# First chunk of a fused recommender kernel: tiles selected by 0/1 matmuls, dummy matmuls, loads issued two parts at a time

## The reference, cut to what matters

```python
e = stack([tbl_f[ids[:, f]] for f in range(39)], axis=1)     # (512, 39, 16)
x0 = xk = e
for idx, (W, b) in enumerate(((w0, b0), (w1, b1), (w2, b2))):
    z = relu(einsum('bhd,bkd,hks->bsd', x0, xk, W) + b[None, :, None])
    if idx != 2:
        xk = z[:, :64, :];  direct.append(z[:, 64:, :])
    else:
        direct.append(z)
z = sum(concatenate(direct, axis=1), axis=-1)
h = relu(concatenate([z, dense_ctx], axis=1) @ W_top1 + b_top1)
y = relu(h @ W_top2 + b_top2) @ W_top3
```

## Time and profile before

| | us |
|---|---|
| median of 3 runs (641.41 to 642.8) | 641.43 |
| profiled execution, device time | 643.21 |
| its span, first to last instruction | 641.4 |
| PE busy | 601.1 (94%) |
| DVE busy | 550.5 (86%) |
| POOL busy | 462.4 (72%) |
| ACT busy | 302.9 (47%) |
| mean granted TensorE clock | 0.987 |

### The profile page before, as it was taken

The page is one execution under the profiler, slowest core; times in us unless marked ns, Lnnn a source line. Parts: engine busy times, 40 slices in busy tenths (PEclk is TensorE's granted clock), DMA queues, the critical chain, the costliest instruction groups (busy, mean ns, idle before and its releaser), DMA issues.

```text
span 641.4 us, 7217 instructions
## 1 busy us (share of the span) xinstructions
PE 601.1 (94%) x1916; PEld 362.1 (56%) x1916; DVE 550.5 (86%) x509; ACT 302.9 (47%) x374; POOL 462.4 (72%) x293
## 2 busy tenths in 40 slices
PE   0258999999999999999999999999999999999998
PEld 0024565666666665656666665656566666656463
DVE  1456999999999999999999999999999999999540
ACT  2023555546454646445364546454454545455313
POOL 6807787878878787878878787878788787647230
PEclk9978999999999999999999999999999999999998
DMA  6798788796959494968769494959787693922000
GB/s 231 170 209 192 160 186 178 167 196 150 210 126 218 95 220 102 219 129 187 162 151 210 109 217 100 219 107 201 143 191 169 138 221 90 219 56 70 2 0 0
DMA packets 28431, 98.13 MB, mean 153 GB/s; under 512 B 8033, under 2 KB 16993, under 8 KB 20354
## 3 DMA queue, kind: packets, MB, share of 16 engines
q1 hardware_dynamic: 21297, 93.44, 66.0%
q0 software_dynamic: 5120, 1.32, 1.9%
q10 hardware_dynamic: 2001, 3.24, 1.5%
HBM read 94.14 MB, written 3.84 MB: 153 GB/s over the span
## 4 chain that ended last, share of the span: by engine, by line
PE 92%; DMA 2%; POOL 2%; DVE 2%; ACT 1%; issue 1%; SPq 1%; DVEq 0%; ACTq 0%
PE z L585 42%; PE z L591 13%; PE z L596 13%; PE z L593 13%; PE z L575 4%; PE z L579 2%; PE z L578 2%; PE d_products L649 1%; POOL gathered L397 1%; DMA x_rep<-x_rows 1%; DVE products L451 1%; PE z L624 1%; POOL low L342 0%; SPq L304 0%; DMA gathered<-in_tables,rows_sb 0%
## 5 line engine op out<-in xcount | busy, mean ns | idle before, releaser
L342 POOL TENSOR_TENSOR low<-products,high 128x1024 fp32r<-128x1024 f32 x128 | 303.9, 2391 | 112.8 <-ACT high L689 101.8
L451 DVE TENSOR_TENSOR products<-x_rep,xk 128x1024 f32<-128x1024 f32 (+1 forms) x258 | 333.0, 1337 | 25.8 <-ACT xk L673 17.9
L585 PE MATMUL z<-products,w_whole 128*128 128x512 f32 x640 | 301.6, 602 | 30.5 <-DVE products L451 30.5
L585 PEld LDWEIGHTS z<-products,w_whole 128*128 128x128 f32 x640 | 122.8, 192 | 136.3 <-issue 121.7
L689 ACT ACTIVATE high<-products 128x1024 fp32r<-128x1024 f32 x128 | 134.8, 1055 | 134.3 <-DVE products L451 121.8
L397 POOL DMA_INDIRECT gathered<-in_tables,rows_sb x160 | 157.8, 986 | 44.4 <-issue 41.3
L591 PE MATMUL z<-high,w_high 128*128 128x512 f32 x352 | 184.4, 524 | 2.6 <-ACT high L689 2.6
L593 PE MATMUL z<-high,w_low 128*128 128x512 f32 x352 | 138.9, 395 | 0.0
L596 PE MATMUL z<-low,w_high 128*128 128x512 f32 x352 | 110.1, 394 | 1.4 <-POOL low L342 1.3
L591 PEld LDWEIGHTS z<-high,w_high 128*128 128x128 f32 x352 | 66.7, 189 | 40.9 <-issue 24.8
L593 PEld LDWEIGHTS z<-high,w_low 128*128 128x128 f32 x352 | 66.7, 190 | 37.5 <-issue 26.8
(11 more groups left out here) (41 smaller groups left out, 156.2 us busy)
## 6 DMA issues: line engine op xcount, KB each, us to landing
x_rep<-x_rows SPq DMA_DIRECT2D x60, 768.0 KB, 14.9
x_rep<-x_rows SPq DMA_DIRECT2D x62, 512.0 KB, 6.4
x_rows<-gathered SPq DMA_DIRECT2D x15, 225.0 KB
x_rep<-x_rows SPq DMA_DIRECT2D x8, 384.0 KB, 8.3
x_rep<-in_w ACTq DMA_DIRECT2D x2, 1280.0 KB, 9.6
gathered<-in_tables,rows_sb POOLq DMA_INDIRECT x160
x_same<-x_rows SPq DMA_DIRECT2D x15, 78.0 KB
x_same<-x_rows SPq DMA_DIRECT2D x16, 64.0 KB
```

The lines of the kernel that those rows point to most:

```text
L342: ops.tensor_tensor(low[0:p, slot, 0:n, :], product(index, p, n), high[0:p, slot, 0:n, :].bitcast(fp32), ALU.subtract).then_inc(low_by[kin ...
L451: nc.vector.tensor_tensor(slots, rep, row.unsqueeze(1).broadcast_to([p, n, N]), ALU.mult).then_inc(made, 1 + pair)
L585: mm = nc.tensor.matmul(out, w_whole[0:p, at, i, :], product(index, p, n)[:, i, :], start=(first and i == 0), stop=(last and i == n - 1))
```

## The change

FIRST_PARTS becomes six parts, of which tiles 4 and 5 come first. The other tiles of layer 0 (SELECTED: 0, 1, 6, 2, 3) are, for the first chunk only, no longer read from `x0_rep`: PE multiplies `x0_same` by a 128 x 128 matrix of zeros and ones for each, so that the row wanted on each partition appears in a PSUM bank (`select`), and DVE multiplies that bank by `x0_same` (`multiply_selected`), one tile at a time. The five matrices are a new input `sel`, loaded by ACT's queue behind w1 and w2 into ring slot 0 of `products`. PE gets three dummy matmuls ahead of the selections, started when the gathers of chunk 0 are done, and three behind layer 0 (`keep_busy`). SP issues part q only once part q - 2 has landed, from part 3 on. The write of chunk 1's rows moves from ACT, behind the roundings of layer 0, to SP, between parts 4 and 5. `load_same(sp, 1)` gets a wait for the last product of layer 0.

```diff
-FIRST_PARTS = [(0, 2), (2, 4), (4, T0), (T0, 10), (10, 14), (14, 17), (17, T1)]
+FIRST_PARTS = [(4, 6), (0, 4), (6, 10), (10, 14), (14, 17), (17, T1)]
+SELECTED = [0, 1, 6, 2, 3]
+SEL_SLOT = 0
+WARM = min(WHOLES.index(i) for i in LAYER0 if i in WHOLES)
+        selector = products[:, SEL_SLOT, :, :].rearrange("p a n -> p (a n)")[:, 0:len(SELECTED) * S] \
+            .rearrange("p (t s) -> p t s", s=S)
+        selected_in = [z[1], z[2], xk[0], xk[1]]
-        HELD = 5
+        HELD = 3
+        WRITTEN_AFTER = 4
             for q in range(1, len(FIRST_PARTS)):
-                if q == HELD:
+                if q >= HELD:
                     sp.wait_ge(first_loaded[q - 2], 32)
                 for e in range(2):
                     load_replicated(sp, 0, e, FIRST_PARTS[q], first_loaded[q])
+                if q == WRITTEN_AFTER:
+                    write_x0(sp, 1)
             sp.wait_ge(x0_written, 16 * WRITES * 2)
             sp.wait_ge(x0_ready, 1)
+            sp.wait_ge(made, count("all", -1, N1 + N0 - 1))
             load_same(sp, 1)
...
+            def multiply_selected(index):
+                _, t, n, (p, *_), _ = BODY[index]
+                out = product(index, p, n)
+                for i in range(n):
+                    at = SELECTED.index(t + i)
+                    dve.wait_ge(selected, at + 1)
+                    done = nc.vector.tensor_tensor(out[0:p, i, :], selected_in[at % len(selected_in)][0:p, :],
+                                                   x0_same[0:p, :], ALU.mult)
+                done.then_inc(made, 1)
...
+            def keep_busy(times):
+                for _ in range(times):
+                    nc.tensor.matmul(z[2][:, :], w_whole[:, WARM, 0, :],
+                                     w_whole[:, WARM:WARM + 2, :, :].rearrange("p w t s -> p (w t s)"), start=True, stop=True)
+            def select(at):
+                nc.tensor.matmul(selected_in[at % len(selected_in)][:, :], selector[:, at, :], x0_same[:, :],
+                                 start=True, stop=True).then_inc(selected, 1)
             everything = range(len(BODY))
+            pe.wait_ge(w_copied, sum(i in WHOLES or i in SPLIT for i in LAYER0))
+            pe.wait_ge(gather_done[0], 16 * GB)
+            keep_busy(3)
+            pe.wait_ge(sel_loaded, 16)
+            pe.wait_ge(same_loaded, 16 * len(ANCHORS))
+            for at in range(len(selected_in)):
+                select(at)
             pe.wait_ge(w_copied, len(WHOLES) + len(SPLIT))
             pe.wait_ge(w_stack_made, len(STACKS))
-            body(-1, LAYER0)
+            body(-1, LAYER0[:1])
+            for at in range(len(selected_in), len(SELECTED)):
+                pe.wait_ge(made, count("all", -1, N1))
+                select(at)
+            body(-1, LAYER0[1:])
+            keep_busy(3)
             body(0, everything)
...
+            act.dma_start(selector, sel).then_inc(sel_loaded, 16)
             act.dma_start(bt1_sb[:, :], bt1).then_inc(biases_loaded, 16)
...
-            write_x0(act, 1)
             after_layer0(-1)
```

More of the change, by code:

```diff
@@ L60 @@
 PARTS = [(0, 4), (4, 8), (8, 14), (14, T1)]
-FIRST_PARTS = [(0, 2), (2, 4), (4, T0), (T0, 10), (10, 14), (14, 17), (17, T1)]
-assert all(row_of(1, end - 1) - row_of(1, first) == end - 1 - first for first, end in PARTS)
+FIRST_PARTS = [(4, 6), (0, 4), (6, 10), (10, 14), (14, 17), (17, T1)]
+SELECTED = [0, 1, 6, 2, 3]
+assert all(row_of(1, end - 1) - row_of(1, first) == end - 1 - first for first, end in PARTS + FIRST_PARTS)
 def parts_new(index, parts):
@@ L130 @@
 LOW_LAG = 1
+SEL_SLOT = 0
+assert all(RINGED.index(i) % RING != SEL_SLOT for i in LAYER0 if i in RINGED)
+WARM = min(WHOLES.index(i) for i in LAYER0 if i in WHOLES)
 LATE = (LOW_DVE, STACKED, ALONE)
@@ L176, in dlrm_cin_kernel @@
 def dlrm_cin_kernel(nc, ids, base, tables, dense, w0a, w0b, b0, bx0, w1, b1, bx1, w2, b2,
-                    wt1, bt1, wt2, bt2, wt3, out):
+                    wt1, bt1, wt2, bt2, wt3, sel, out):
     fp32, fp32r, i32 = mybir.dt.float32, mybir.dt.float32r, mybir.dt.int32
@@ L258, in dlrm_cin_kernel @@
         biases_loaded = sem("biases_loaded")
+        sel_loaded = sem("sel_loaded")
+        selected = sem("selected")
         x0_ready = sem("x0_ready")
@@ L500, in body @@
                         if isinstance(c, int) and c == -1:
-                            wait_first(index)
+                            if t not in SELECTED:
+                                dve.wait_ge(first_loaded[0], 32)
                         else:
@@ L515, in body @@
                             wait_slot(dve, c, index + 1)
-                        multiply(c, index)
+                        if isinstance(c, int) and c == -1 and t in SELECTED:
+                            multiply_selected(index)
+                        else:
+                            multiply(c, index)
                     if kind in LATE:
@@ L817 @@
     }
+    sel = _np.zeros((S, len(SELECTED), S), _np.float32)
+    for at, t in enumerate(SELECTED):
+        for p in range(S):
+            sel[next(q for q in range(S) if anchor_of(q) == field_of(p, t)), at, p] = 1
+    arrays["sel"] = sel
     nc = _bacc.Bacc("TRN2", target_bir_lowering=False, num_devices=1)
```

## The result

| | us |
|---|---|
| after, median of 20 runs (639.17 to 642.38) | 641.13 |
| before, median of 20 runs beside them (640.19 to 644.56) | 642.79 |
| after : before | 0.9975 [0.9965, 0.9985] |
| profiled execution of after, device time | 640.96 |
| its span | 639.2 |

The change makes the kernel 1.7 us faster, 0.25%, which lies within the 0.3% that the forecast called the same. The forecast was 639.1 us; the 641.13 us lie above the 637.9 to 640.9 us that its main theory allowed, and within the wider range. Two numbers have to be kept apart in what follows: the level of before, which was 641.43 us in the three runs at hand and is 642.79 us in twenty, of which those three are the first, and the gain, forecast as 2.3 us and measured as 1.66.

What follows compares the result with a forecast made beforehand. PE bounds on average, but the end hangs on x0_same of chunk 1: 2.4 us earlier, less 0.1 selector and 0.1 clock, 2.2 rounded up to 2.3 us; median 641.43 becomes 639.1 us, range 637.0 to 642.2.

Steps and rivals of the forecast that it cites:

- main theory: Whole kernel: earlier x0_same of chunk 1 brings it to 639.1 us, own range 637.9 to 640.9, chance 0.55.
- The bound and the mechanism: Chunk 0 on PE: the end moves with index 13's start, held by ACT awaiting x0_same of chunk 1; 70.56 becomes 68.2 us.
- The step that failed first: the level: Whole kernel: the gain is taken off a median of 641.43 us, giving 639.1 us.
- The term that was mis-sized: x0_same: Chunk 1's x0_same reaching ACT: lands at 49.5 us instead of 51.87, 2.4 us earlier.
- The clock term: PE from index 3 of chunk 0: low clock after its wait costs 0.1 us more, bounds 0.6 gain to 1.5 loss.
- The reason given for the 2.4 us: SP's queue: the write of chunk 1's rows goes behind part (14, 17) among the loads, so x0_same is issued at 45.3 us.
- The rival that the gathers hold SP: Chunk 1's gathers: loads sharing the engines delay them and so SP's write; 640.5 to 643.7 us, chance 0.20.
- The estimate from it: Chunk 1's gathers: with engines taking turns one packet at a time they are done at 40.1 us, and the sum stands.
- The write did not overtake the loads: Rival on SP's queue: small packets are served ahead of earlier parts, x0_same lands at about 46 us; 636 us, chance 0.07.
- the selections found the clock up: Rival in layer 0 of chunk 0: the clock stays low for the selections, layer 0 ends at about 42 us; 640 us, chance 0.08.
- The change does nothing that counts: Rival for the whole kernel: gathers or selector late by as much as x0_same gains; 641 us, chance 0.10.
- as the prediction said of layer 0: Layer 0 of chunk 0: ends 7.3 us earlier, worth nothing by itself since PE then waits for ACT.

Runs made afterwards that it cites:

- second pair: The changed kernel, unchanged, timed again beside the kernel before on the same chip: 641.05 us against 642.99, ratio 0.9974.
- the filled gap: The change plus six dummy matmuls ahead of index 3 of chunk 0 and one between its high and low parts: 639.48 us against 642.99, 0.9949.
- first experiment: The kernel before with only the write of chunk 1's rows moved from ACT to SP, behind part (14, 17): 638.94 us against 642.48, 0.9952.
- before, again 1: The kernel before, unchanged, a second profiled execution: device time 638.77 us.
- before again 1, 3 and 4: The kernel before, unchanged, its second, fourth and fifth profiled executions: device times 638.77, 642.72 and 642.63 us.
- before, again 2: The kernel before, unchanged, one more profiled execution: device time 640.99 us.

## Why the prediction was right or wrong

**The bound and the mechanism: right.** The chain of steps came as told. x_bank at 49.50 us (49.5 told), SP's write at 39.60 (39.7 to 42), layer 0 ended at 36.0 (35.3), PE's index 0 at 38.81 (37.9), one gap in PE of 5.19 us ended by ACT's rounding of index 3 (6 us), index 13 at 68.32 (68.2), DVE waiting in layer 1 for tile 17 alone (1.46 us; 3 told). The head of that execution was 0.5 us late from its fourth gather on (1.55 us where it takes 0.94), which is most of the 0.9 us in index 0. The DMA engines showed no gap between 40 and 47 us (95% busy or more in each microsecond). The profiled pair differs by 643.21 - 640.96 = 2.25 us against 2.3. That it agrees so closely is partly luck: the sum was made in one execution of before, and after's own three executions spread over 0.7 us in x_bank and in index 13.

Two slips on the way cost nothing. Indices 0 to 2 from 37.9 us on, by the terms given, end at 43.7 us and not 44.7; they ended at 45.9, since PE also waited for ACT and POOL. And the write of chunk 1's rows is 407 packets in the trace, not 384.

**The step that failed first: the level.** "... the median of the runs, 641.43 us, becomes 639.1 us." The text had beside it a profiled execution of 643.21 us and made the whole sum in that execution, but then took it off a median of three, of which two lay at 641.4. Twenty runs, those three among them, have 642.79, and before's medians beside the experiments were 641.98 to 642.99: 1.36 of the 2.03 us by which the forecast missed.

**The term that was mis-sized: x0_same.** 51.87 us was taken as the kernel's value, while it is one draw of a number that runs from 50.46 to 52.53 us. The mean of five is 51.5, of three after 49.5: 2.0 us, not 2.4. Index 13 moves from a mean of 70.0 to 67.9 us, 2.1 us, which is rough, for before's five lie between 67.81 and 71.73. The timed gain is 1.66 us, and 1.94 us in the second pair; the remaining 0.2 to 0.4 us can be the kernel's end, below, which is open. The second part of the miss is this term, 0.67 us with that remainder (the forecast took off 2.33, the runs show 1.66).

**The clock term.** "0.1 us lost" is near: in the profiled pair it is 14.73 against 14.59 us from the low part of index 3 to index 13, and on average 14.34 after against 14.42 before. But its meaning was not seen. Against the 13.26 us that the work takes with the clock kept, before pays 1.3, 2.7 and 1.8 us in 3 of the 5 executions and nothing in two, after 1.5, 0.5 and 1.3 in 3 of 3. In the change it is paid every time because the faster layer 0 makes PE wait for the rounding of index 3 every time; how long it waits matters less, since without dummies a wait of 1.20 us cost about as much (14.59 us, 1.3 over). The profiled executions of the moved write and of the filled gap both keep the clock. The filled gap is 1.6 us faster than the change beside it; the moved write gains 3.5 us on its before where the change gains 1.7 to 1.9.

**The reason given for the 2.4 us: half right.** The prediction put it down to the write's place in the loads' order, and gave the hold no share. The write alone does give x_bank at 49.20 us (first experiment, with early gathers); but with the hold the write on ACT's queue does nearly as well (49.78 us), and without it on ACT's queue it gives 51.75. The reading that fits these single executions is that it counts how many loads are in flight when the write is to move, and that either part of the change sees to it.

**The rival that the gathers hold SP: fell.** gather_done[1] came at 39.60 us with 8 KB packets in flight, as before with mixed ones. In 34 to 36 us of after, the queues moved

```profile
q1 hardware_dynamic: 67, 0.42, 95.5%
q0 software_dynamic: 109, 0.03, 10.7%
```

109 of the gathers' packets to 67 of the loads'. The rule that the prediction weighed, of the Trainium skill, "DMA: Bandwidth & Descriptors", "Queues, rings and completion order", that an engine takes turns a packet at a time, does not give these counts if one record of the trace is one packet; the same section of the Trainium skill lets a packet hold several descriptors, and which of them the trace counts no run here shows. The estimate from it, 40.1 us, was near the measured 39.60.

**The other rivals.** The write did not overtake the loads, and the selections found the clock up (1.95 us for two products). "The change does nothing that counts" is true of its most visible parts: layer 0 7 us earlier, five selections and six dummies are worth nothing that the runs can tell from zero (1.0018 [0.9998, 1.0038] without hold and moved write), as the prediction said of layer 0.

## What to carry to other kernels

Time won ahead of a wait is only a longer wait, and on PE a longer wait can cost the clock behind it: ask of each step that gets faster what PE then does until the next release, and fill that gap or don't open it. When a small transfer decides, look at how much is in flight ahead of it on all queues, and move or hold that before rebuilding the computation; here one moved write (0.9952) gave at least as much as the whole change (0.9975). Before a sum of 2 us is taken off a median, the median needs more than three runs and each moving term more than one execution.

## What was not expected of the hardware

- An indirect gather's issue on POOL mostly takes 0.94 to 0.97 us, but one of chunk 1's ten takes 4.06 or 4.07 us in 3 of the 5 executions of before and 3.19 us in a fourth. In the short case a copy on DVE that runs meanwhile takes 0.48 us instead of 0.28, as if the two excluded each other and chance decided who goes first. DVE of "before, again 1":

```profile
21.16 0.48 DVE L543 COPY w_whole<-x_rep 128x256 f32<-128x256 f32 x1
```

  The Trainium skill, "SBUF — State Buffer", "SBUF: two separate sides", tells of such a lock between DVE's two-port operations and GpSimd; the rows fit it, and no run here tests it.
- The kernel's end has two lengths. From index 13 of chunk 0 to the end of the span it is 569.1 us in some executions (before again 1, 3 and 4, the moved write, the filled gap) and 570.8 in others, after always among the latter. The difference lies between 626 and 633 us, where the last layers' small matmuls are. Windows of "before, again 1" and "before, again 2":

```profile
628.00:630.00 2.00, 2.00 (x6) 0.95 (x5) 0.00 (x0) 0.00 (x0) 0.00 (x0) 1.00 0.00 0
```

```profile
628.00:630.00 2.00, 2.00 (x4) 0.81 (x3) 0.00 (x0) 0.01 (x1) 0.00 (x0) 0.55 0.00 0
```

  No edit touches that stage. In the profiled execution of after the head's loss (some 7 us at the lower level) and this one (some 3.4 us) are together 5.2 us of clock in 639, which is its mean of 0.992; this one alone would leave 0.997. Of after's 20 timed runs 19 have a mean of 0.992 or less, of the filled gap's twelve eight have 0.997 and four 1.00. So after seems to lose the clock at the end nearly always, while before kept it there in 3 of 5 executions, and that is worth the 0.2 to 0.4 us that the head's gain has over the timed one, or more. Why the head should bear on the end is open; it was not tried.
- The granted clock says what is allowed, not yet how fast PE goes. It is shown as 1.00 from 18 to 23 us of after, while the three dummies (six records) take 5.18 us, some 1.7 us each, the time of the lower level; from 24.28 us on two products take 1.95 us. A window of a microsecond among the dummies:

```profile
20.00:21.00 1.00, 1.00 (x3) 0.41 (x2) 1.00 (x5) 0.00 (x0) 0.69 (x2) 1.00 0.31 60
```
